# Graph kernel, counts stage: records of edges fetched by SyncE and taken apart by ScalarE instead of GpSimd

## The reference, cut to what matters

```python
edge_index = jnp.stack([src, dst])
x = _layernorm(x + _L0_gnn_ref(x, edge_index, L0_gnn_gamma), axis=-1)          # 10 steps of propagation
x = _layernorm(x + _L1_gnn_ref(x, L1_gnn_qW, L1_gnn_kW, L1_gnn_vW, src, dst), axis=-1)   # attention
x = _layernorm(x + _L2_gnn_ref(x, L2_gnn_weights, L2_gnn_loop_w, L2_gnn_bias, src, dst, edge_type_8), axis=-1)
x = _layernorm(x + _L3_gnn_ref(x, ...), axis=-1)

# in _L0_gnn_ref:
deg = jax.ops.segment_sum(jnp.ones((src.shape[0],), x.dtype), dst, num_segments=n)
def prop(h):
    return jax.ops.segment_sum(h[src] * norm, dst, num_segments=n)
```

## Time and profile before

| | us |
|---|---|
| runs, median of 3 (lowest to highest) | 2582.21 (2578.12 to 2589.15) |
| the profiled execution: its own time | 2571.02 |
| its span, first to last instruction | 2569.3 |
| the changed stage in it | 43.6 to about 482 |

### The profile page before, as it was taken

One profiled execution on the slowest core, in us unless ns is written; L12 is line 12 of the kernel. 1 busy time (PEld: TensorE's weight loads), 2 busy tenths in 40 slices (PEclk: granted clock), 3 DMA queues, 4 the chain that ended last, 5 costly groups with the idle time before them and its releaser, 6 DMA issues. The chain is left out here.

```text
span 2569.3 us, 63293 instructions
## 1 busy us (share of the span) xinstructions
PE 2173.7 (85%) x22329; PEld 1800.9 (70%) x22330; DVE 2047.2 (80%) x3355; ACT 1038.6 (40%) x2085; POOL 709.7 (28%) x1336
## 2 busy tenths in 40 slices
PE   3788778799999998676777767899998999999897
PEld 2777777699999998211111213799898599989787
DVE  8888888765555664799999996799888699888546
ACT  1666666432333332699999995100000400000223
POOL 3655555200000000100000001466663266666000
PEclk8999999899999999799999997999999999999899
DMA  2333333211000100511111114332223423223610
GB/s 77 132 150 150 145 129 150 110 40 41 28 27 32 35 27 8 137 41 41 42 42 42 41 38 156 106 85 72 80 74 58 175 71 85 72 71 58 248 79 20
DMA packets 95191, 206.49 MB, mean 80 GB/s; under 512 B 21620, under 2 KB 61172, under 8 KB 94880
## 3 DMA queue, kind: packets, MB, share of 16 engines
q1 hardware_dynamic: 80544, 182.39, 20.3%
q0 software_dynamic: 14464, 21.44, 4.5%
HBM read 118.17 MB, written 84.76 MB: 79 GB/s over the span
## 5 line engine op out<-in xcount | busy, mean ns | idle before, releaser
L1816 PE MATMUL l_bank<-tab,mask 128*128 128x192 f16 x7600 | 653.5, 247 | 38.9 <-issue 30.0
L1816 PEld LDWEIGHTS l_bank<-tab,mask 128*128 128x128 f16 x7600 | 628.8, 98 | 59.7 <-issue 58.2
L1404 DVE TENSOR_SCALAR mask<-code 128x1600 int32<-128x1600 int32 x304 | 538.3, 1812 | 78.6 <-remote 39.0
L1788 POOL DMA_INDIRECT ggot<-table_dram,gidx x432 | 411.6, 953 | 240.9 <-issue 84.0
L1287 DVE SCALAR_TENSOR_TENSOR pr<-ex,cring 128x1568 f32<-128x1568 f32 x200 | 356.6, 1784 | 10.0 <-DMA cring<-c_dram 10.0
L1233 PE MATMUL att_acc<-pr,v 128*32 128x392 f32 x1600 | 184.8, 535 | 146.9 <-DVE pr L1287 138.1
L836 PE MATMUL sums<-onehots,ct 128*128 128x192 f16 x3125 | 263.6, 247 | 10.4 <-DVE onehots L902 6.3
L836 PEld LDWEIGHTS sums<-onehots,ct 128*128 128x128 f16 x3125 | 260.5, 98 | 13.4 <-issue 6.9
L836 PE MATMUL sums<-u,ct 128*128 128x192 f16 x3125 | 259.1, 246 | 0.0
L836 PEld LDWEIGHTS sums<-u,ct 128*128 128x128 f16 x3125 | 258.0, 98 | 0.0
L1261 ACT ACTIVATE ex<-score_rest,poss 128x1176 f32<-128x1176 f32 x200 | 248.7, 1244 | 2.8 <-PE score_rest L1225 2.6
(11 more groups left out here) (342 smaller groups left out, 3188.9 us busy)
## 6 DMA issues: line engine op xcount, KB each, us to landing
code<-code_dram SPq DMA_DIRECT2D x38, 800.0 KB
code_dram<-flat SPq DMA_DIRECT2D x100, 200.0 KB, 1.9
ct_dram<-ct SPq DMA_DIRECT2D x25, 800.0 KB, 4.0
c_dram<-flat SPq DMA_DIRECT2D x25, 800.0 KB, 3.4
ct_again<-ct_dram SPq DMA_DIRECT2D x25, 800.0 KB, 17.5
cring<-c_dram SPq DMA_DIRECT2D x200, 98.0 KB, 1.9
table_dram<-tab SPq DMA_DIRECT2D x50, 384.0 KB, 2.3
flat<-code_dram SPq DMA_DIRECT2D x19, 800.0 KB, 4.3
```

Of the source, the lines that this page charges most:

```text
L1404: e.tensor_scalar(turned.rearrange("p (s q d) -> p s q d", q=NQ, d=DQ // 2), words.rearrange("p (q s d) -> p s q d", q=NQ, d=DQ // 2), abs ...
L1788: e.indirect_dma_start(ggot[:, k, j, :], None, table_dram[:, :], bass.IndirectOffsetOnAxis(ap=gidx[:, k, j:j + 1], axis=0)).then_inc(s_ggo ...
L1816: mm = e.matmul(acc[k][:, 0:2 * D], mask[:, r % MR, s, :], tab[:, s, r, :], start=(r == 0 and s == 0), stop=(r == R - 1 and s == NT - 1))
```

## The change

The edges become records of 8 bytes: the two halves and the float32 column side by side in `edge_rec`. The two shifting DMAs of the setup move twice the bytes each, and there are two in place of four.

The block of GpSimd is gone. SyncE reads the table, waits for `s_col` and issues two DMAs for each step, which copy three records of each partition (24 bytes in each of 128) into a slot of `rec`, four slots in turn (`RECS`). Its stores stand between these, five windows later than their data's window (`LAG`). ScalarE waits for the slot's semaphore and for `s_code`, copies the halves into `sel` and the columns with the bias `woff` into `col`, one instruction each (`chosen`). Two offsets in one bias are possible since the pattern `iota` is now made in three parts, with the second half's offset in it. ScalarE copies a window's sums out two windows behind (`window_out(t, w - 2)`) instead of one. [...]

The diff, cut to its core:

```diff
-        edge_col = edges[:, 0:2 * NCHP]
-        edge_sv = edges[:, 2 * NCHP:].bitcast(F16).rearrange("p (c k) -> p c k", k=2)
+        edge_rec = edges[:].rearrange("p (c k) -> p c k", k=2)
+        edge_col = edge_rec[:, :, 1]
+        edge_sv = edges[:].bitcast(F16).rearrange("p (c k) -> p c k", k=4)[:, :, 0:2]
...
-                @block.gpsimd
...
-                                    first = load(e, tile_tab[0:1, bass.ds(t, 1), 2 * w + h], 0, 2 * NCHP - GRP)
...
-                                e.wait_ge(s_code, e.snap(free) + 1)
-                                for h in range(2):
-                                    ins = e.tensor_copy(sel[:, w % 2, :, h * GRP:(h + 1) * GRP],
-                                                        edge_sv[:, bass.ds(chunks[h], GRP), :].rearrange("p g c -> p c g"))
-                                ins.then_inc(s_sel, 1)
-                                for h in range(2):
-                                    ins = e.tensor_tensor(col[:, w % 2, h * GRP:(h + 1) * GRP], edge_col[:, bass.ds(chunks[h], GRP)],
-                                                          woff[:, bass.ds(t * WPS + (2 * w + h), 1)].to_broadcast([P, GRP]), ALU.add)
-                                ins.then_inc(s_col, 1)
...
+                    def chosen(t, w, groups, of):
...
+                        with e.Fori(0, groups):
+                            e.wait_ge(s_rec[of][w % RECS], e.snap(taken[w % RECS]) * 32 + 32)
+                            e.wait_ge(s_code, e.snap(free) + 1)
+                            e.activation(sel[:, w % 2, :, :], rec_sv[:, w % RECS, :, 0:2].rearrange("p g c -> p c g"),
+                                         ACT.Copy).then_inc(s_sel, 1)
+                            e.activation(col[:, w % 2, :], rec[:, w % RECS, :, 1], ACT.Identity,
+                                         bias=woff[:, bass.ds(t * WPT + w, 1)]).then_inc(s_col, 1)
...
+                            chosen(t, w, groups, of)
+                            if w >= 2:
+                                window_out(t, w - 2, first)
...
+                    def records(t, w, groups, of):
...
+                        with e.Fori(0, groups) as g:
...
+                                first = load(e, tile_tab[0:1, bass.ds(t, 1), 2 * w + h], 0, 2 * NCHP - GRP)
...
+                            e.wait_ge(s_col, e.snap(free) + 1)
+                            for h in range(2):
+                                e.dma_start(rec[:, w % RECS, h * GRP:(h + 1) * GRP, :].rearrange("p g c -> p (g c)"),
+                                            edge_rec[:, bass.ds(chunks[h], GRP), :].rearrange("p g c -> p (g c)")).then_inc(s_rec[of][w % RECS], 16)
...
+                    def stored(t, w, before, rows):
+                        for q in range(NQ):
+                            due = 2 * q + 1 + LAG
+                            if due == w:
+                                quarter(t, q)
+                            elif due == w + WPT and before:
+                                quarter(t - 1, q)
+                                if q == NQ - 2 and rows:
+                                    row(t - 2)
+                                if q == NQ - 1:
+                                    own(t - 1)
```

More of the change, by code:

```diff
@@ L598, in row_out @@
                                      ACT.Copy, accum_out=dacc[:, bass.ds(t, 1), q]).then_inc(s_turn_out, 1)
-                    def tile(t, first, second):
+                    e.sem_inc(s_code, 1)
+                    n, past, free = three(e, "act")
+                    taken = [e.alloc_register(f"cnt_act_taken{k}") for k in range(RECS)]
+                    def chosen(t, w, groups, of):
+                        e.reg_mov(free, past)
+                        e.reg_mov(past, n)
+                        with e.Fori(0, groups):
[5 more added lines that the diff above has]
+                                         bias=woff[:, bass.ds(t * WPT + w, 1)]).then_inc(s_col, 1)
+                            e.reg_add(taken[w % RECS], taken[w % RECS], 1)
+                            e.reg_add(n, n, 1)
+                            e.reg_mov(free, n)
@@ L601, in tile @@
+                    def tile(t, of, first, second, last=False):
+                        groups = groups_of(e, t)
                         for w in range(WPT):
[L602 to L603 removed]
+                            chosen(t, w, groups, of)
+                            if w >= 2:
+                                window_out(t, w - 2, first)
                             elif not first:
[L605 removed]
@@ L606, in tile @@
-                            if not first and w - 1 in turned_after:
-                                row_out(t - 1, turned_after[w - 1], second)
-                    tile(0, True, False)
-                    tile(1, False, True)
-                    with e.Fori(2, NT - 1) as t:
-                        tile(t, False, False)
+                                window_out(t - 1, WPT - 2 + w, second)
+                            if not first and w - 2 in turned_after:
+                                row_out(t - 1, turned_after[w - 2], second)
@@ L614, in root @@
+                            if last and w == 2:
+                                root(0)
                     def root(i):
@@ L616, in root @@
                         e.activation(dinv[:, PARTS[i]], rdeg[:, PARTS[i]], ACT.Sqrt).then_inc(s_sqo, 1)
-                    root(0)
-                    tile(NT - 1, False, False)
+                    for of in range(len(s_rec)):
+                        for r in taken:
+                            e.reg_mov(r, 0)
+                        if of == 0:
+                            tile(0, of, True, False)
+                            tile(1, of, False, True)
+                            tile(2, of, False, False)
+                        elif of < NT // SPAN:
+                            with e.Fori(SPAN * of, SPAN * of + SPAN) as t:
+                                tile(t, of, False, False)
+                        else:
+                            tile(NT - 1, of, False, False, True)
+                    window_out(NT - 1, WPT - 2, False)
                     window_out(NT - 1, WPT - 1, False)
@@ L628, in _ @@
                 def _(e):
-                    def tile(t, first):
-                        for q in range(NQ):
-                            if q == NQ - 1 and not first:
-                                row(t - 1)
-                            e.wait_ge(s_out, t * WPT + 2 * (q + 1))
-                            e.dma_start(code_dram[bass.ds(t, 1), :, q, :, :].rearrange("o p s d -> (o p) (s d)"),
-                                        stage[:, q % 2, :, :].rearrange("p s d -> p (s d)")).then_inc(s_stored[q % 2], 16)
+                    e.sem_inc(s_col, 1)
@@ L641, in row, with tile @@
                         e.dma_start(c_dram[bass.ds(t, 1), :, :].rearrange("o p n -> (o p) n"), crow).then_inc(s_row_out, 16)
-                    tile(0, True)
-                    with e.Fori(1, NT) as t:
-                        tile(t, False)
+                    def stored(t, w, before, rows):
[9 more added lines that the diff above has]
+                                    own(t - 1)
+                    def tile(t, of, before, rows):
+                        groups = groups_of(e, t)
+                        for w in range(WPT):
+                            records(t, w, groups, of)
+                            stored(t, w, before, rows)
+                    tile(0, 0, False, False)
+                    tile(1, 0, True, False)
+                    tile(2, 0, True, True)
+                    for of in range(1, NT // SPAN):
+                        with e.Fori(SPAN * of, SPAN * of + SPAN) as t:
+                            tile(t, of, True, True)
+                    tile(NT - 1, NT // SPAN, True, True)
+                    for w in range(LAG):
+                        stored(NT, w, True, True)
                     row(NT - 1)
```

95 lines of the change are left out of this document (53 added, 42 removed).

## The result

The changed kernel took **2852.7 us** (median of 4 runs, 2848.5 to 2855.3) against 2581.1 of the kernel before (4 runs): a ratio of 1.104, 95% interval 1.102 to 1.107. The forecast was 2722 us and its range ended at 2790. So the direction and the engine that sets the pace were forecast rightly, and the size was not: +272 us where +140 was expected.

What follows compares the result with a forecast made beforehand. GpSimd's sequencer was taken to bound the counts stage, SyncE's queue after the change: 22.6 us a tile against 17.06, 25 x 5.54 = 138, +2 for landing, so 2582 + 140 = 2722 us; range 2635 to 2790 us.

Steps and rivals of the forecast that it cites:

- The issue: SyncE's issue of one record DMA with its register operation: 0.50 us, two in each step.
- Long reads: SyncE's table reads lasting over 280 ns: 1.2 of GpSimd's 1.4 us a tile for these and true waits stays.
- Rest of a step: Reads, registers, branch and wait of a SyncE step, priced from GpSimd's chain: 1.25 us, 2.20 for the step after shortening.
- Stores: Four code stores, a ct store and a c store a tile in SyncE's queue: 0.53 us each, 3.2 us.
- Overhead: SyncE's own cost per tile, one more read and the loop: 0.6 us, against 0.86 on GpSimd.
- The backlog rival: SyncE's issues lengthen behind the stores: 25 us a tile, +200 us, 2782 us; chance 0.15.
- Lean SyncE: SyncE's short register operations give 19.3 to 20.5 us a tile, 2640 to 2668 us; chance 0.12.
- SyncE no bound: Reads cost SyncE's queue nothing; VectorE and TensorE set 13.5 us a tile, 2493 us; chance 0.07.
- ScalarE the bound: SyncE fast, ScalarE's small copies set 17.4 us a tile: +8 us, 2590 us; chance 0.03, shared with near-equality.
- DMAs and landing: Record DMAs take at most 1.7 us a step and land in time, four slots covering 11 us: no bound.
- TensorE's clock: Lower clock likelier with longer waits; 20.6 us a tile then, still under 22.6, so no cost.
- Setup: Two larger shifts and three GpSimd patterns instead of one: some 5 us more on GpSimd, zero on the total.

Runs made afterwards that it cites:

- e1: Changed kernel with one DMA of six records a step instead of two of three; the unused second read was left out too: ratio 1.017.
- e2: Changed kernel with one read of the table a step, its chunk serving both DMAs: ratio 1.065.
- e3: Changed kernel with the six stores of a tile issued by GpSimd, SyncE keeping the records: ratio 1.065.
- e5_forms: Changed kernel with other DMA forms in place of the records in six of eight windows from tile 3; only issue durations measured, 496 ns in the control.
- g3: Changed kernel with GpSimd fetching records by two copies a step, no DMA, both chunk numbers in one word, two setup patterns made later: ratio 0.971.
- u1: Kernel before with one part of the change alone, the sums copied two windows late: ratio 1.003.

## Why the prediction went wrong, point by point

**What bounds the kernel after: right.** SyncE waits for 0.7 us of 670, the others wait for it, and what three edits took from its tile came back in the stage: 9.1, 4.1 and 4.4 us a tile, and 9.0, 4.0 and 4.2 by the stage's length (e1, e2, e3).

**The step: the terms that failed.** SyncE's tile was put at 22.6 us and is 28.0 once the stores run beside it (27.5 over the whole stage, 683.8 / 199 x 8). Its account from the trace of after, tiles 4 to 21, each instruction counted from its start to the start of the next:

| term, us a tile | forecast | measured |
| --- | --- | --- |
| 16 record issues with their register operation | 8.0 (0.50 each) | 11.0 (0.539 + 0.148) |
| rest of eight steps, a read taken as 0.285 | 9.6 | 10.4 |
| six stores with their register operations | 3.2 | 3.7 |
| the tile's overhead: one read, the loop | 0.6 | 0.7 |
| long reads, beyond 0.285 us each | 1.2 | 2.2 |
| sum | 22.6 | 28.0 |

*The issue* is the largest, 3.0 of the 5.4 us: "so 0.50 for each" was taken from stores, whose destination is DRAM. The record's is SBUF, and e5_forms shows this form at 0.50 us of bare duration. Its nearest row was in the prediction's hands: the setup's first shift, from `edges` to `edges`, SBUF to SBUF, took 0.56 us. It was read as the start of a backlog and put into a rival. With it, an issue would have been put at 0.56 + 0.17 = 0.73 us (an estimate after the fact; 0.69 was measured), the tile at 22.6 + 16 x 0.23 = 26.3, and the change at +233 us: 2815 us instead of 2722.

*Long reads:* "the same reads are made beside the same stores, so 1.2 of it stays" subtracted too much: 2.2 us stay, and half of this goes when the stores are issued elsewhere (e3). *Rest of a step:* 1.29 us where 1.20 was taken. GpSimd's step stood model for it, and SyncE's turns over four registers (`past`, L651, 0.15 us) where GpSimd's line for that took 0.07 (L419). *Stores:* the 0.53 is from two stores with no sum for a wait between them; the register operations that work out what each wait is for (L668, L677) cost 0.45 us a tile more. *Overhead:* nearly right, 0.7 for 0.6; the code is written out for every three tiles (`SPAN`), each set with semaphores of its own (`[of]`).

**The backlog rival** gave 25 us a tile and a chance of 0.15: its size was nearer, its mechanism wrong. An issue takes 496 ns in the median with stores in SyncE's queue and 494 without (e3), and without them more of the issues were long, not fewer. Its sign ("if the stage is over 640 us, the backlog holds") came, with 683.8 us, from another cause: a length alone doesn't tell one rival from another. As the rival also made the upper bound of the range ("If eight of the issues of a tile, behind the two 800 KB stores, take 0.3 us more"), this bound raised half of the issues where the form raises all 16, and ended at 2790 us.

**Lean SyncE, SyncE no bound, ScalarE the bound:** none came. That a stage whose records come fast enough runs a tile in 13.5 us was right and is g3; 17.4 us for ScalarE was an upper bound, at least 3.9 too high.

**DMAs and landing: right.** 1.7 us after issue, the ring never full, "no bound".

**TensorE's clock: right to cost nothing**; it did fall, to 0.69 over the stage.

**Setup: "Zero" was wrong**, by 4.0 us. The argument looked only at who reads the patterns and not at which of VectorE's instructions run at the same time. The first record added 2.2 us more, as forecast.

**The late copy of sums: nearly right**, 0.3% where nothing was forecast (u1).

## What to carry to other kernels

A DMA is not free for the engine that issues it: count each issue with its register operations as serial work, and price it by a row with the same source and destination, since into SBUF it cost 0.69 us where a store cost 0.62. When a helper's chain of reads and small instructions is the bound, shorten the chain (fewer reads, half of the instructions, the rest on an engine with room) before moving it to another queue: here the first gave 3.2%, the second cost 10.4%. And where work is added to GpSimd, look which of VectorE's instructions run beside it.

## What had not been expected of the hardware

- SyncE's issue of 24 B a partition: 496 ns into SBUF, 344 ns into DRAM. Two of them took 1.17 to 1.20 us into SBUF from either source and 0.86 into DRAM, and 1.30 with 64 and 16 partitions in the place of 128 (e5). No cause was found.
- An issue with no register operation ahead of it lasted 602 ns where one behind such an operation lasted about 495, and the pair took the same 1.13 to 1.14 us (e2, after): a small register operation between two issues can be free, and single durations sum only roughly.
- A pattern of GpSimd's (2.3 us) and a cast or scale of VectorE (0.6 us alone, 1.06 into the records) hold each other: 2.3 to 2.7 us for the latter.
- A read of one word into a register took 260 ns in the median and up to 872; moving six stores a tile to another engine took away half of what the long ones cost (e3).
